# A two-layer graph and expert kernel: counting tables moved from setup into the first front stage, x loaded in pieces, aggregation in column halves, another finishing order

## The chip, the cores and the metric

One core of a Trainium2 chip runs the whole program. The metric is the device time in microseconds (us) of one execution; lower is better. The engines are named as the profile names them: PE is TensorE (PEld its weight loads), DVE is VectorE, ACT is ScalarE, POOL is GpSimd, SP is SyncE; a q behind a name (SPq, ACTq) is the engine's own sequencer, which also issues DMAs. L456 is line 456 of the kernel before.

## The reference

A graph of 3750 nodes and 60000 edges sorted by destination goes through two layers. x has 512 features for each node, 8 heads of 64.

```python
def gat_multihead(h, src, dst, Wfc, Wa):
    z = jnp.einsum('ni,hoi->nho', h, Wfc)
    e = leaky_relu(s_src[src] + s_dst[dst])          # s_*: z times a_src / a_dst, per head
    ex = jnp.exp(e - segment_max(e, dst)[dst])
    alpha = ex / segment_sum(ex, dst)[dst]
    return segment_sum(alpha[:, :, None] * z[src], dst).reshape(N, 512)
...
x = x + ffn(elu(gat(ln(x))) + ln(x))                 # layer 0: attention, FFN 512-256-512, layer norm
x = x + experts_choice(ln(x))                        # 16 experts, each takes its 468 best nodes
x = x + ln(gat1(ln(x), edge_type, edge_weight) + ln(x))
x = x + moe_top2(ln(x))                              # 8 experts, top 2 for each node
```

## The kernel before

The program is a row of stages, each with its own blocks and with a barrier at its end: setup, then for each layer front, aggregate and finish, and after them the expert stages. Nodes are held as 30 tiles of 128 rows; edges as 235 groups of 256 (J = 2 columns of 128), 15 groups for each of 16 chunks.

**setup** (L115 to L300). SP loads all of x (L168), then the edge lists, and writes -1e30 over the table first_scores in HBM (L174). POOL makes constants. DVE splits dst into a low and a high part, makes 30 pairs of one-hot matrices (L254, L255, each pair for 16 columns), and PE multiplies them (L295, 16 matmuls a pair) into a histogram of destinations. From this DVE works out first_edge (L259 to L269: the edge at which each node begins), then in 29 steps the group in which each tile ends (L272) and in 29 more the tables of the aggregation's steps (L278, L279): step_group, step_tile, group_freed, neg_base.

**front** (L335 on). SP loads the weights. DVE: stats of x in batches of 6 tiles (L474), normalise (L332), weights times attention vectors (L495, L496). PE turns the normalised tiles (L572) and scores them (L578), 16 columns a tile; DVE copies the scores out (L507, L508, the semaphore s_copied), makes a bf16 table of them (L513, L516) and, in layer 0, marks where a node's edges begin and end with six passes over the whole edge list (L524 to L529). Then PE does the big product z (L603, 4 matmuls of 512 columns a tile, each of which the trace shows as two instructions, as it does all f32 matmuls); ACT copies it out (L673) and SP stores it. Meanwhile POOL scatters 30 tiles of destination scores to first_scores (L456), one indirect DMA a tile, and then picks source scores for 5 groups of each chunk, 160 indirect DMAs (L464).

The remaining source scores are picked on PE, in a loop of m = 0 to 79: DVE makes one-hots (L553), PE selects from the table (L635, 6 matmuls), DVE masks (L562), PE spreads (L644, for m-1). Into this loop TURNS_AT puts 20 "turn blocks" (L625), transposes that bring scores to the form of the edges: ("g", i) for POOL's picks, ("d", n) for the scores read back from first_scores. ACT's order is: the z copies, wait for all of z, wait for all 30 scatters, 10 DMA issues that read first_scores back in 5 pairs (load_dst, L657), then one copy for each turn block (L685, and L690 at the end), with more load_dst pairs between. PE may not start turn block m (m > 0) before ACT has copied block m-1. After the loop: scans, exponentials and a turn back (alpha).

**aggregate** (L785 to L914), 264 steps. A step is one group of edges against one node tile. POOL gathers the z rows of a group with 2 indirect DMAs (L848), into 8 slots, SP passing on freed slots (L856). ACT prepares rel, alp and scale from alpha (L826, L828, L829) and evicts a bank of a finished tile (L814). DVE makes two one-hots (L879) and the messages (L882: gathered rows times alpha, which it reads from PSUM). PE opens a bank (L897), then for each of 2 columns multiplies one-hot by 512 message columns (L911) and, into a separate bank of denominators, by 8 alpha columns (L913). Four PSUM banks go round; LATE = 4 steps pass before a bank is evicted.

```python
for r in range(RING):
    t = pe.value_load(k.step_tile[0:1, bass.ds(i * RING + (r + LATE), 1)], ...)      # L906
    pe.wait_ge(evicted, i * RING + (r + LATE)); open_bank(...)
    pe.wait_ge(msg_ready, i * RING + (r + 3))
    # J times: matmul 512 columns (L911), matmul 8 columns (L913)
    mm.then_inc(summed, 1)
```

**finish_layer0**, 10 blocks of 3 tiles. DVE per block n: join (L1046, L1048), renew (L963), divide(n+2) (L1041), close(n) (L1053 to L1057, moments L936, then add_branch with the reciprocal L948 that needs ACT's root). ACT: renorm(n-1), norm(n+2) (L1087), expo(n+2) (L1092, L1093), hidden(n+1) (L1105), root(n) (L970, a square root), then the copies of x turns (L1098). PE: second(n) (L1179), y turn (L1155), hidden(n+1) (L1170), x turn (L1155), logits (L1187).

**experts0** ends with a block of its own that loads all of x again from x_rows (L1661).

Of the kernel before, what the change touches and what calls it, by code (L numbers as in the profile page):

```python
# [13 lines left out]
I32 = mybir.dt.int32  # L14
# [28 lines left out]
TURNS_AT = {**{4 + 4 * n: ("d", n) for n in range(GC - 1)}, 78: ("d", GC - 1), **{m: ("g", i) for i, m in enumerate((6, 13, 33, 53, 76))}}  # L43
# [6 lines left out]
NBK = 4  # L50
LATE = 4
# [63 lines left out]
def setup(k, I):  # L115

    nc = k.nc
    with ExitStack() as ctx:
        sem = lambda n: nc.alloc_semaphore(name="setup_" + n)
        sb = lambda n, s, d: ctx.enter_context(nc.sbuf_tensor("setup_" + n, s, d))  # L120
        loaded, x_padded, dve_done, pe_done, chain_sem, pool_chain = (
            sem("loaded"), sem("x_padded"), sem("dve_done"), sem("pe_done"), sem("chain"), sem("pool_chain"))
        d_filled, onehots_ready, onehots_used, table_read, table_stored = (
            sem("d_filled"), sem("onehots_ready"), sem("onehots_used"), sem("table_read"), sem("table_stored"))
        dst_i = sb("dst_i", [P, NG * J], I32)
        lo_i = sb("lo_i", [P, NG * J], I32)
        lo = sb("lo", [P, NG * J], BF16)
        hi = sb("hi", [P, NG * J], BF16)
        TO = 16
        oh_lo = sb("oh_lo", [P, 2, TO, P], BF16)  # L130
        oh_hi = sb("oh_hi", [P, 2, TO, NT], BF16)
        lowest = sb("lowest", [P, (EPAD + NPAD) * H // P], F32)
        hist = sb("hist", [P, NT], F32)
        incl = sb("incl", [P, NT], F32)
        first = sb("first", [P, NT], F32)
        dump = sb("dump", [P, NT], F32)
        empty = sb("empty", [P, NT], F32)
# [3 lines left out]
        kk = sb("kk", [P, STEPS], F32)  # L141
        g256 = sb("g256", [P, NGR - 1], F32)
        cmp = sb("cmp", [P, NGR - 1], F32)
        kt = sb("kt", [P, NT - 1], F32)
        ones_row = sb("ones_row", [P, NT], F32)
        steps_i = sb("steps_i", [P, 2, STEPS], I32)
        kg = sb("kg", [P, NT - 1], F32)
        group_at = sb("group_at", [P, NGR], F32)
        freed = sb("freed", [P, NGR], F32)
        ck = sb("ck", [P, STEPS], F32)  # L150
        q7 = sb("q7", [P, P], F32)
        spread_at = sb("spread_at", [P, HT * H + P], F32)
        src_i = sb("src_i", [P, NG * J], I32)
        part_i = sb("part_i", [P, 2, NG * J], I32)
        part = sb("part", [P, 2, NG * J], BF16)
        node_part = sb("node_part", [P, 2, NG * J], F32)
        upper = sb("upper", [P, NG * J], F32)
        parts_ready, parts_stored = sem("parts_ready"), sem("parts_stored")
        shifts = sb("shifts", [P, 30], I32)
        one_i = sb("one_i", [P, 30], I32)  # L160
        NOH = NG * J // TO

        with nc.Block() as block:
            @block.sync
            def _(sp):
                sp.wait_ge(x_padded, 1)
                sp.dma_start(k.x[:, 0:NT - 1, :], I["x"][0:(NT - 1) * P, :].rearrange("(t p) d -> p t d", p=P)).then_inc(loaded, 16)
                sp.dma_start(k.x[0:N - (NT - 1) * P, NT - 1, :], I["x"][(NT - 1) * P:N, :]).then_inc(loaded, 16)  # L168
                sp.dma_start(dst_i[:, :], I["dst_groups"]).then_inc(loaded, 16)
                sp.dma_start(k.src_groups[:, :], I["src_groups"]).then_inc(loaded, 16)  # L170
                sp.dma_start(k.src_chunks[:, :], I["src_chunks"]).then_inc(loaded, 16)

                sp.wait_ge(d_filled, 1)
                sp.dma_start(k.first_scores.rearrange("(p r) h -> p (r h)", p=P), lowest[:, :]).then_inc(table_stored, 16)  # L174
                sp.wait_ge(table_stored, 16)
                sp.dma_start(src_i[:, :], I["src_list"].rearrange("(p n) -> p n", p=P)).then_inc(loaded, 16)
                sp.wait_ge(loaded, 96)

            @block.gpsimd
            def _(pool):  # L180
                chain = Chain(pool, pool_chain)
                g = nc.gpsimd
                g.memset(k.x[:, NT - 1, :], 0.0).then_inc(x_padded, 1)
                g.memset(lowest[:, :], -BIG).then_inc(d_filled, 1)
                g.memset(k.ones[:, :], 1.0)
                g.memset(one_i[:, :], 1)
# [7 lines left out]
                g.iota(k.iota[:, :], pattern=[[1, P]], base=0, channel_multiplier=0, allow_small_or_imprecise_dtypes=True)  # L194
                g.iota(k.tile_iota[:, :], pattern=[[1, NT]], base=0, channel_multiplier=0, allow_small_or_imprecise_dtypes=True)
                g.iota(dump[:, :], pattern=[[P, NT]], base=EPAD, channel_multiplier=1, allow_small_or_imprecise_dtypes=True)
                g.iota(gate_i[:, :], pattern=[[0, 1]], base=0, channel_multiplier=1)
                g.iota(kk[:, :], pattern=[[1, STEPS]], base=0, channel_multiplier=0, allow_small_or_imprecise_dtypes=True)
                g.iota(g256[:, :], pattern=[[GE, NGR - 1]], base=GE, channel_multiplier=0, allow_small_or_imprecise_dtypes=True)
                g.iota(group_at[:, :], pattern=[[1, NGR]], base=0, channel_multiplier=0, allow_small_or_imprecise_dtypes=True)  # L200
                g.iota(spread_at[:, :], pattern=[[1, HT * H + P]], base=-HT * H, channel_multiplier=0, allow_small_or_imprecise_dtypes=True)
                g.iota(q7[:, :], pattern=[[0, CH], [1, H]], base=0, channel_multiplier=0, allow_small_or_imprecise_dtypes=True)
                g.iota(k.node[:, :], pattern=[[P, NT]], base=0, channel_multiplier=1, allow_small_or_imprecise_dtypes=True)
                chain(g.iota(shifts[:, :], pattern=[[-1, 30]], base=29, channel_multiplier=0))

        with nc.Block() as block:
            @block.sync
            def _(sp):

                sp.wait_ge(parts_ready, 1)  # L210
                sp.dma_start(k.src_key.rearrange("(p n) -> p n", p=P), part[:, 0, :]).then_inc(parts_stored, 16)
                sp.dma_start(k.src_tile.rearrange("(p n) -> p n", p=P), part[:, 1, :]).then_inc(parts_stored, 16)
                sp.wait_ge(parts_stored, 32)

            @block.vector
            def _(dve):
                v = nc.vector
                chain = Chain(dve, chain_sem)
                v.tensor_single_scalar(part_i[:, 0, :], src_i[:, :], P - 1, ALU.bitwise_and)
                chain(v.tensor_single_scalar(part_i[:, 1, :], src_i[:, :], 7, ALU.logical_shift_right))  # L220
                chain(v.tensor_copy(node_part[:, :, :], part_i[:, :, :]))
                chain(v.tensor_scalar(upper[:, :], node_part[:, 1, :], float(HT), None, ALU.is_ge))
                v.scalar_tensor_tensor(part[:, 0, :], upper[:, :], float(P), node_part[:, 0, :], ALU.mult, ALU.add)
                v.scalar_tensor_tensor(part[:, 1, :], upper[:, :], -float(HT), node_part[:, 1, :], ALU.mult, ALU.add).then_inc(parts_ready, 1)
# [110 lines left out]
def front(k, name, layer, I, w_dram, a_src_dram, a_dst_dram):  # L335
# [3 lines left out]
    with ExitStack() as ctx:  # L339
# [63 lines left out]
        with nc.Block() as block:  # L403
# [162 lines left out]
            def _(pe):  # L566
# [24 lines left out]
                for n in range(LEAD):  # L591
                    turn(n)
# [1510 lines left out]
```

## Time and profile before

| | |
|---|---|
| median of 3 runs | 4148.77 us (4142.35 to 4155.31) |
| profiled execution, own time | 4150.25 us |
| its span | 4148.7 us |
| mean granted PE clock | 0.868 |
| PE busy | 3108.9 us (75%) |
| DVE busy | 2261.3 us (55%) |
| POOL busy | 1616.9 us (39%) |
| ACT busy | 1099.6 us (27%) |

By the stretches of the timeline the stages lie so: setup 0 to 172 us, front of layer 0 to 636 (its second block from 571), aggregate 636 to 1290, finish_layer0 to 1583, choice of tokens and experts to 2309, front of layer 1 2311 to 2779, aggregate 2780 to 3430, the rest to 4149. A share of busy time is a mean over stages that have different limits, so it says little about any one edit: each stage is read by itself.

### The profile page before, as it was taken

The numbers are of one execution on the slowest core, as the hardware profiler recorded it, in microseconds if no ns is written. First come the engines' busy times: TensorE is split into PE (matmuls) and PEld (weight loads), VectorE is DVE, ScalarE is ACT, GpSimd is POOL, SyncE is SP. The second block draws the span as 40 slices with busy tenths as digits, with TensorE's granted clock in tenths as the row PEclk, the third lists the DMA queues.
The fourth block names the chain that finished last, engine by engine and source line by source line (L and its number), as shares of the span: only waits on it lengthen the run. The fifth ranks groups of instructions, "written<-read, shape, count | busy, mean of one in ns | idle before, by whom it ended". The sixth has DMA issues, their size and how long they took to land. (4 is left out here: it accounts for less than half of the span.)

```text
span 4148.7 us, 59841 instructions
## 1 busy us (share of the span) xinstructions
PE 3108.9 (75%) x12040; PEld 1861.1 (45%) x12041; DVE 2261.3 (55%) x4019; ACT 1099.6 (27%) x3080; POOL 1616.9 (39%) x1660
## 2 busy tenths in 40 slices
PE   1298958999997773389998599939999994308990
PEld 1174524555554552354444554515555553305660
DVE  6841577777776665731111413587777779712224
ACT  0021003444444440011111110014444444204440
POOL 0037706766761000013333067317776650140116
PEclk9999978999998785579999589969999995559995
DMA  2115616766662110035554426417666654053326
GB/s 106 35 43 130 172 39 178 203 192 195 192 192 71 53 56 29 0 106 154 144 156 101 130 72 152 121 37 210 199 196 193 193 163 183 23 214 133 121 106 226
DMA packets 334037, 541.05 MB, mean 130 GB/s; under 512 B 173220, under 2 KB 178596, under 8 KB 333168
## 3 DMA queue, kind: packets, MB, share of 16 engines
q0 software_dynamic: 118624, 327.53, 28.1%
q1 hardware_dynamic: 91472, 208.44, 14.5%
q10 hardware_dynamic: 123840, 3.94, 1.7%
q8 instruction: 40, 0.66, 0.1%
q14 instruction: 61, 0.50, 0.0%
HBM read 427.14 MB, written 112.61 MB: 130 GB/s over the span
## 5 line engine op out<-in xcount | busy, mean ns | idle before, releaser
L911 PE MATMUL bank<-aggregate_msg,aggregate_onehot 128*128 128x512 f32 x2112 | 1163.8, 639 | 20.4 <-issue 8.4
L848 POOL DMA_INDIRECT aggregate_zg<-z_rows,src_groups x940 | 890.4, 947 | 602.0 <-issue 267.9
L882 DVE TENSOR_TENSOR aggregate_msg<-aggregate_zg,bank 128x1024 f32<-128x1024 f32 x528 | 638.4, 1209 | 4.5 <-SPq L860 4.5
L913 PEld LDWEIGHTS bank<-aggregate_alp,aggregate_onehot 128*128 128x128 f32 x2112 | 402.4, 191 | 507.4 <-issue 507.4
L879 DVE TENSOR_SCALAR aggregate_onehot<-bank,aggregate_rel 128x128 f32<-128x128 f32 x1056 | 321.6, 346 | 362.2 <-PE bank L913 355.4
L814 ACT COPY acc<-bank x536 | 314.2, 586 | 358.0 <-issue 349.7
L464 POOL DMA_INDIRECT front_d<-src_scores,src_chunks x320 | 304.7, 952 | 97.6 <-issue 97.6
L1561 POOL DMA_INDIRECT exp_xg<-hn_rows,exp_gather_tok x64 | 67.0, 1048 | 705.1 <-DVE exp_gather_tok L1585 540.8
L911 PEld LDWEIGHTS bank<-aggregate_msg,aggregate_onehot 128*128 128x128 f32 x2112 | 318.8, 191 | 35.7 <-issue 28.7
L913 PE MATMUL bank<-aggregate_alp,aggregate_onehot 128*128 128x8 f32 x2112 | 300.8, 215 | 0.0
L826 ACT ACTIVATE aggregate_rel<-dst_groups,neg_base 128x2 f32 x528 | 156.0, 295 | 394.8 <-PE bank L913 288.2
L635 PE MATMUL bank<-front_w,front_table 128*120 128x512 bf16 x960 | 240.5, 388 | 9.0 <-DVE front_w L553 9.0
L456 POOL DMA_INDIRECT first_scores<-s_dst,first_edge x60 | 82.0, 1366 | 403.7 <-DVE s_dst L508 386.0
L1652 PE MATMUL bank<-exp_w,exp_h_t 128*117 128x512 f32 x512 | 222.5, 592 | 0.7 <-ACT exp_h_t L1619 0.7
L1644 PE MATMUL bank<-exp_xg_t,exp_w 128*128 128x468 f32 x512 | 206.0, 561 | 0.6 <-ACT exp_xg_t L1612 0.6
L635 PEld LDWEIGHTS bank<-front_w,front_table 128*120 128x120 bf16 x960 | 130.1, 136 | 153.3 <-issue 101.8
L603 PE MATMUL bank<-front_w,front_edge 128*128 128x512 f32 x360 | 169.4, 608 | 0.0
L644 PE MATMUL bank<-front_z,spread 120*128 120x512 f32 x320 | 166.3, 601 | 0.1
L572 PE MATMUL bank<-ident,front_early 128*128 128x128 f32 x240 | 64.7, 429 | 125.2 <-DVE front_early L332 105.6
L1572 POOL DMA_INDIRECT x_rows<-exp_y,exp_add_tok x64 | 101.2, 1581 | 141.9 <-DVE exp_y L1600 106.8
L1867 POOL DMA_DIRECT2D slot_out<-exp_y x66 | 35.8, 542 | 303.0 <-DVE exp_y L1884 303.0
L1644 PEld LDWEIGHTS bank<-exp_xg_t,exp_w 128*128 128x128 f32 x512 | 98.1, 192 | 106.8 <-issue 105.8
(365 smaller groups left out, 4356.1 us busy)
## 6 DMA issues: line engine op xcount, KB each, us to landing
exp_w<-in_L_ffn_w SPq DMA_DIRECT2D x32, 1024.0 KB, 8.2
slot_in<-alpha SPq DMA_DIRECT2D x1, 16896.0 KB, 43.5
exp_xin<-slot_in SPq DMA_DIRECT2D x66, 256.0 KB, 2.8
slot_out<-exp_y POOLq DMA_DIRECT2D x66, 256.0 KB, 2.3
z_rows<-front_z SPq DMA_DIRECT2D x60, 256.0 KB, 2.0
aggregate_zg<-z_rows,src_groups POOLq DMA_INDIRECT x940, 3.7
front_early<-src_key SPq DMA_DIRECT2D x16, 640.0 KB, 4.7
front_early<-src_tile SPq DMA_DIRECT2D x16, 640.0 KB, 4.5
```

The source lines that it names most:

```text
L464: pool.indirect_dma_start(picked[:, at:at + H], None, k.src_scores[:, :], bass.IndirectOffsetOnAxis(k.src_chunks[:, n:n + 1], 0)).then_inc ...
L603: mm = nc.tensor.matmul(k.ps[3 + n % 2][:, :], hn_t(c, slice(n * P, (n + 1) * P)), w[:, c, :], start=(c == 0), stop=(c == KC - 1))
L635: mm = nc.tensor.matmul(k.ps[5 + m % 2][0:HT * H, :], parts[:, part, half, :], onehot[:, m % OH, half, :], start=(part == 0 and half == 0) ...
L644: nc.tensor.matmul(sums[b], k.spread[0:HT * H, at:at + P], masked[0:HT * H, (m - 1) % 2, :], start=(c == 0), stop=(c == CH - 1)).then_inc( ...
L814: nc.scalar.copy(k.acc_all[:, bass.ds(t, 1), :].rearrange("p a d -> p (a d)"), flat[:, bass.ds(((t + (NBK - 1)) & (NBK - 1)) * 512, 512)]) ...
L848: pool.indirect_dma_start(zg[:, r, j, :], None, k.z_rows[:, :], bass.IndirectOffsetOnAxis(k.src_groups[:, n:n + 1], 0)).then_inc(gathered[ ...
L879: v.tensor_scalar(onehot[:, m, j, :], lanes, rel[:, r, j:j + 1], None, ALU.is_equal)
L882: v.tensor_tensor(msg[:, m, :, :].rearrange("p j (h d) -> p (j h) d", h=H), z, bcast_last(scale[r % 2], DH), ALU.mult).then_inc(msg_ready, 1)
L911: nc.tensor.matmul(flat[:, bass.ds((t & (NBK - 1)) * 512, 512)], onehot[:, m, j, :], msg[:, m, j, :], start=False, stop=True, skip_group_c ...
L913: mm = nc.tensor.matmul(flat[:, bass.ds(t * H + den, H)], onehot[:, m, j, :], alp[:, r, j * H:(j + 1) * H], start=False, stop=True, skip_g ...
L1644: mm = nc.tensor.matmul(k.ps[f][:, 0:CAP], w1[:, u, c, f * P:(f + 1) * P], xg_t[:, c, :], start=(c == 0), stop=(c == KC - 1))
L1652: mm = nc.tensor.matmul(k.ps[4 + q][0:PQ, :], h_t[:, f, q * PQ:(q + 1) * PQ], w2[:, u, f, :], start=(f == 0), stop=(f == F - 1))
```

## The change

Six edits, in one step:

- setup keeps only constants. In layer 0 the histogram, first_edge and the step tables are made inside front: one-hots and count matmuls lie among the z matmuls, count_ends and count_steps in the loop over m (at m = 4 to 32 and m = 35 to 63). The fill of first_scores is issued in front too, from z's buffer.
- front loads x itself, in 5 pieces of 6 tiles, and each batch of stats waits for its piece, in both layers. The block that loads x again after experts0 is gone.
- POOL makes 96 of its 160 picks first, then the 30 scatters, then the other 64 picks. TURNS_AT is another. ACT's order is the same.
- aggregate: the message row is 4 pieces of 260 columns (256 of message, 4 of alpha), so a step has 4 matmuls of 260 columns and none of 8; tiles alternate between two pairs of banks, and an eviction comes one step after (LATE = 1). ACT makes no rel and no alp; DVE's one-hot takes step_base and dst_groups at addresses from a register.
- the denominators are in acc_all, so their reciprocal waits for the last eviction.
- finish_layer0: ACT's order is root(n), hidden(n+1), expo(n+2), norm(n+2); DVE's close is split into receive (before divide) and close; PE does second(n+1) right after hidden(n+1).

```diff
-TURNS_AT = {**{4 + 4 * n: ("d", n) for n in range(GC - 1)}, 78: ("d", GC - 1), **{m: ("g", i) for i, m in enumerate((6, 13, 33, 53, 76))}}
+PICKS_BEFORE = 3
+TURNS_AT = {**{19 + 4 * n: ("d", n) for n in range(GC - 1)}, 76: ("d", GC - 1), **{m: ("g", i) for i, m in enumerate((4, 9, 14, 34, 50))}}
-LATE = 4
+LATE = 1
+HW = HD + H // 2
@@ front, SP
+                load_x(0)
                 sp.dma_start(w[:, :, :], ...)
...
+                for b in range(1, NT // SBT):
+                    load_x(b)
@@ front, POOL
+                if layer == 0:
+                    nc.gpsimd.memset(k.x[:, NT - 1, :], 0.0).then_inc(x_padded, 1)
+                    nc.gpsimd.memset(z[:, :, :], -BIG).then_inc(filled, 1)
+                    pool.wait_ge(lists_loaded, 32)
+                pool.wait_ge(s_stored, 16)
+                for i in range(PICKS_BEFORE):
+                    pick(i)
+                if layer == 0:
+                    pool.wait_ge(first_ready, 1)
+                    pool.wait_ge(table_filled, 16)
+                for n in range(NT):
+                    pool.indirect_dma_start(k.first_scores[:, :], ...)
+                for i in range(PICKS_BEFORE, GS):
+                    pick(i)
@@ front, DVE, layer 0
+                    for b in range(NOH):
+                        if b >= 2:
+                            dve.wait_ge(onehots_used, b - 1)
+                        v.tensor_tensor(oh_lo[:, b % 2], ..., ALU.is_equal)
+                        v.tensor_tensor(oh_hi[:, b % 2], ..., ALU.is_equal).then_inc(onehots_made, 1)
+                    dve.wait_ge(onehots_used, NOH)
...
+                    chain(v.tensor_copy(k.first_edge[:, :], first))
+                    dve.sem_inc(first_ready, 1)
                     (the six passes over the edge list follow)
                 for m in range(PICKS + 1):
+                    if layer == 0 and 4 <= m < 4 + NT - 1:
+                        count_ends(m - 4)
+                    if layer == 0 and 5 + NT <= m < 5 + NT + NT - 1:
+                        count_steps(m - 5 - NT)
@@ front, PE
+                    if layer == 0 and n >= 4:
+                        count(n - 4)
...
+                    for b in range(NT - 4, NOH):
+                        count(b)
+                    pe.wait_ge(first_ready, 1)
@@ aggregate, ACT
+                def evict(n): ... act.wait_ge(summed, n + (RING - 1)); copy(acc_all[t*2 : +2], banks[((t+1)&1)*2 : +2, 0:HW])
+                def prepare(n, r): ... act.wait_ge(summed, n + (RING - MS + 1)); copy(msg[.., HD:HW], coef); copy(scale[r % 2], coef)
                     for r in range(RING):
                         evict(i * RING + r)
+                        prepare(i * RING + (r + 1), r + 1)
@@ aggregate, PE
-                        pe.wait_ge(evicted, i * RING + (r + LATE))
-                        open_bank(bass.ds(((t + 1) & (NBK - 1)) * 512, 2))
                         pe.wait_ge(msg_ready, i * RING + (r + 3))
                         for j in range(J):
-                            nc.tensor.matmul(..512 columns..); nc.tensor.matmul(..8 columns..)
+                            for half in range(2):
+                                nc.tensor.matmul(k.banks[:, bank(t, half), 0:HW], onehot[:, m, j, :], msg[:, m, j * 2 + half, :], ...)
+                        pe.wait_ge(evicted, i * RING + (r + 3))
+                        open_tile(t + 1).then_inc(summed, 1)
@@ finish_layer0, ACT
-                    if n + 2 < NB:
-                        norm(n + 2)
-                        expo(n + 2)
+                    root(k, act, std[:, :], mv[:, :, 1], var_ready, std_ready, n)
                     if n + 1 < NB:
                         hidden(n + 1)
-                    root(k, act, std[:, :], mv[:, :, 1], var_ready, std_ready, n)
+                    if n + 2 < NB:
+                        expo(n + 2)
+                        norm(n + 2)
@@ finish_layer0, DVE
+                    receive(n)
                     if n + 2 < NB:
                         divide(n + 2)
                     close(n)
@@ experts0
-        with nc.Block() as block:
-            @block.sync
-            def _(sp):
-                sp.dma_start(k.x[:, :, :], k.x_rows.rearrange("(t p) d -> p t d", p=P)).then_inc(b_loaded, 16)
```

## Rows read from the trace of the kernel before

**Rows 1.** Busy time by stretch: us and instructions of each engine, PE clock, DMA share, GB/s.
```profile
0.00:33.00 33.00, 0.00 (x0) 0.01 (x1) 0.02 (x1) 0.02 (x1) 7.49 (x23) 1.00 0.86 318
...
266.00:372.00 106.00, 106.00 (x242) 46.71 (x241) 31.03 (x13) 16.99 (x29) 84.84 (x66) 1.00 0.29 88
372.00:571.00 199.00, 183.06 (x681) 99.25 (x680) 103.97 (x240) 10.32 (x26) 118.85 (x125) 0.96 0.60 153
...
2296.00:2308.00 12.00, 0.00 (x0) 0.00 (x0) 0.00 (x0) 0.00 (x0) 0.00 (x0) 0.50 1.05 387
```

**Rows 2.** Timeline of DVE in setup: start, us, operation.
```profile
122.29 2.28 DVE L254 TENSOR_TENSOR setup_oh_lo<-setup_lo,iota_bf 128x2048 bf16<-128x2048 bf16 x1
124.49 0.65 DVE L255 TENSOR_TENSOR setup_oh_hi<-setup_hi,iota_bf 128x480 bf16<-128x480 bf16 x1
```

**Rows 3.** One line's instructions in setup: duration ns min/median/max, first and last start.
```profile
L279 DVE SCALAR_TENSOR_TENSOR setup_ck<-setup_kk,setup_kt,setup_ck x29: 473/475/476, 144.4 to 169.3; 128x264 f32<-128x264 f32 x29
```

**Rows 4.** Timeline of DVE in the front of layer 0.
```profile
172.81 3.66 DVE L474 BATCH_NORM_STATS2 front_bn<-x 128x6 f32<-128x512 f32 x6 [1.04 <-PEq L2042]
...
266.33 0.41 DVE L507 COPY s_src<-bank 128x240 f32<-128x240 f32 x1 [12.70 <-PE bank L578]
...
268.81 4.20 DVE L524 TENSOR_TENSOR front_e<-front_wide 128x3840 bf16<-128x3840 int32 x1
...
295.44 2.16 DVE L529 TENSOR_SCALAR front_wide<-front_wide 128x7680 bf16<-128x7680 bf16 x1
```

**Rows 5.** Timeline of POOL over the same stretch, with the idle time before each.
```profile
274.15 3.77 POOL L456 DMA_INDIRECT first_scores<-s_dst,first_edge  x1 [0.30 <-issue]
...
298.72 0.96 POOL L456 DMA_INDIRECT first_scores<-s_dst,first_edge  x1 [0.30 <-issue]
```

**Rows 6.** Timeline of the loop over m, all engines.
```profile
396.93 0.69 PE L625 MATMUL bank<-ident,front_edge 128*128 128x128 f32 x2 [8.55 <-DMA front_edge<-first_scores]
...
404.69 2.87 ACTq L657 DMA_DIRECT2D front_edge<-first_scores  x2
...
449.73 0.75 DVE L562 SCALAR_TENSOR_TENSOR front_z<-front_edge,half_tile,bank 120x512 f32<-120x512 bf16 x1 [1.13 <-PE bank L635]
...
454.02 0.75 DVE L562 SCALAR_TENSOR_TENSOR front_z<-front_edge,half_tile,bank 120x512 f32<-120x512 bf16 x1 [0.84 <-PE bank L635]
```

**Rows 7.** Aggregate, 700 to 1200 us: waits (us in total, times, longest).
```profile
ACT acc L814 <- issue: 137.6, 207, 0.7
...
POOL aggregate_zg L848 <- SPq L856: 40.9, 25, 2.1
```

**Rows 8.** Timeline of aggregate around 1000 us.
```profile
1000.29 0.59 ACT L814 COPY acc<-bank  x1 [0.66 <-issue]
...
1001.47 1.12 PE L911 MATMUL bank<-aggregate_msg,aggregate_onehot 128*128 128x512 f32 x2
...
1002.57 0.68 PE L911 MATMUL bank<-aggregate_msg,aggregate_onehot 128*128 128x512 f32 x1
```

**Rows 9.** Costliest groups of the page: count, busy us, mean ns, idle before.
```profile
L848 POOL DMA_INDIRECT aggregate_zg<-z_rows,src_groups x940 | 890.4, 947 | 602.0 <-issue 267.9
L882 DVE TENSOR_TENSOR aggregate_msg<-aggregate_zg,bank 128x1024 f32<-128x1024 f32 x528 | 638.4, 1209 | 4.5 <-SPq L860 4.5
```

**Rows 10.** PE's sequencer at the step's register load, both layers.
```profile
L906 PEldq TENSOR_LOAD <-step_tile x528: 296/302/510, 639.1 to 3423.1; - x176
```

**Rows 11.** Timeline of PE in finish_layer0.
```profile
1512.71 5.43 PE L1170 MATMUL bank<-alpha,fin_w 128*128 128x384 f32 x16 [0.67 <-ACT alpha L1098]
```

**Rows 12.** What DVE's L948 waited for (us, times), whole trace.
```profile
  ACT fin_std L970: 62.6, 9
```

**Rows 13.** Busy time by stretch in finish_layer0, columns as in rows 1.
```profile
1473.30:1500.80 27.50, 20.79 (x77) 13.75 (x77) 19.29 (x31) 14.40 (x20) 0.00 (x0) 0.81 0.15 57
```

**Rows 14.** The timeline where the front of layer 1 begins.
```profile
2286.91 0.39 SPq L1661 DMA_DIRECT2D x<-x_rows  x1
...
2310.93 3.66 DVE L474 BATCH_NORM_STATS2 front_bn<-x 128x6 f32<-128x512 f32 x6 [40.72 <-PEq L2042]
```

More of the change, by code:

```diff
@@ L49 @@
 SLOTS = 8
-NBK = 4
-LATE = 4
+LATE = 1
+HD = D // 2
+HW = HD + H // 2
 AHEAD = 3
@@ L112, with setup @@
     pass
-def setup(k, I):
+def setup(k):
     nc = k.nc
@@ L405, in _, with load_x @@
             def _(sp):
+                def load_x(b):
+                    rows = I["x"] if layer == 0 else k.x_rows
+                    last = NT // SBT - 1
+                    full = SBT - 1 if layer == 0 and b == last else SBT
+                    sp.dma_start(k.x[:, b * SBT:b * SBT + full, :],
+                                 rows[b * SBT * P:(b * SBT + full) * P, :].rearrange("(t p) d -> p t d", p=P)).then_inc(x_loaded[b], 16)
+                    if layer == 0 and b == last:
+                        sp.wait_ge(x_padded, 1)
+                        sp.dma_start(k.x[0:N - (NT - 1) * P, NT - 1, :], rows[(NT - 1) * P:N, :]).then_inc(x_loaded[b], 16)
+                load_x(0)
                 sp.dma_start(w[:, :, :], w_dram.rearrange("(c p) n -> p c n", p=P)).then_inc(loaded, 16)
@@ L453, in _, with pick @@
             def _(pool):
-                pool.wait_ge(s_copied, 2)
-                for n in range(NT):
-                    pool.indirect_dma_start(k.first_scores[:, :], bass.IndirectOffsetOnAxis(k.first_edge[:, n:n + 1], 0),
-                                            k.s_dst[:, n, :], None).then_inc(scattered, 16)
-                pool.wait_ge(s_stored, 16)
-                for i in range(GS):
+                def pick(i):
                     for j in range(J):
@@ L472, in stats @@
                 def stats(b):
+                    dve.wait_ge(x_loaded[b], 32 if layer == 0 and b == NT // SBT - 1 else 16)
                     for j in range(SBT):
@@ L589, in spread_kinds, with count @@
                                      start=True, stop=True).then_inc(kinds_spread, 1)
+                def count(b):
+                    pe.wait_ge(onehots_made, b + 1)
+                    for t in range(TO):
+                        mm = nc.tensor.matmul(k.ps[5][:, 0:NT], oh_lo[:, b % 2, t, :], oh_hi[:, b % 2, t, :],
+                                              start=(b == 0 and t == 0), stop=(b == NOH - 1 and t == TO - 1))
+                    mm.then_inc(onehots_used, 1)
                 for n in range(LEAD):
@@ L801, in aggregate @@
         ROUNDS = STEPS // RING
[L802 to L805 removed]
+        lanes = k.ps[4][:, 0:P]
+        scale = [k.ps[5 + u][:, 0:J * H] for u in range(2)]
         zslots = zg[:, :, :, :].rearrange("p r j d -> p r (j d)")
@@ L2043, in stage @@
                 run(k, *args)
-        stage(setup, I)
+        stage(setup)
         for layer in range(2):
```

369 lines of the change are left out of this document (159 added, 210 removed).

## The prediction

> **What bounds the kernel now.** I read the busy shares first and then by stretch, since no engine is full over the whole span. Setup is DVE's: 30 pairs of one-hots, 2.28 + 0.65 us each [rows 2], after an x load that fills the DMA engines [rows 1]. The z stretch of front is PE's: 106 us busy of 106 [rows 1]. The loop over m is PE's too, 183 of 199 us; DVE has 104 us of work for 80 turns there, 1.3 us each, while the loop's period is (454.02 - 449.73)/2 = 2.15 us [rows 1, 6]. In aggregate no engine is full: 207 evictions in 500 us are 2.418 us a step [rows 7]. PE alone would need about 2.23: 1.10 us from column to column, twice, and the small opening [rows 8]. POOL needs 2 x (0.947 + 0.30) = 2.51 us a group, which over 235 groups and 264 steps is 2.23 a step [rows 5, 9], and was held by SPq for only 41 us in 500 [rows 7]. So the step is a ring: PE's step, DVE's message, ACT's 0.66 us of issue before 0.59 us of eviction [rows 8], PE again. In finish_layer0 a block lasts 27.5 us with DVE busy for 19.3 and PE for 20.8 [rows 13]; DVE waited for ACT's root 62.6 us in 9 blocks [rows 12].
>
> **Setup and the first front stage.** What stays of setup is constants, 7.5 us of POOL [rows 1]. Front's DVE began at 172.8 [rows 4] and would begin at 7.5: -165.3. x must now be loaded inside: before stats(1) can run, two pieces of 1.57 MB, 1.05 MB of weights and 0.52 MB of vectors land; at 387 GB/s [rows 1] that is 12.2 us and 2 for issue and latency, where stats(1) ran 4.1 after the start. That is +10; I take 10.3. Bounds: 4 (the first piece alone) and 20 (the whole of x). Scores were copied 93.5 us after the start [rows 4]: now at 111.3.
>
> Then the counting. PE does 16 small matmuls per z tile, an estimated 0.45 us with both kinds full, on top of 3.5 us a tile [rows 1]: 30 tiles end at about 229. DVE needs 2.28 + 0.65 = 2.93 less overlap, 2.77 a pair, so it keeps up. The last four counts and the 12 small operations to first_edge cost 12: 241.7. The six passes over the edges ran from 268.81 to 297.60, 28.8 us [rows 4], beside the z matmuls, which hid them. Now they come after the one-hots and stand open: 270.5. PE's first selection follows at 272.2, where before it was at 376.9. So on this path the gain is 105 us.
>
> **POOL's order gives part of it back.** POOL picks from about 114. The rows show what DVE does to it: a scatter took 3.77 us beside L524, which reads two inputs from SBUF and took 4.20, against 0.96 once the passes had ended [rows 4, 5]. The one-hots have that form too, so I take it that one pick can pass during a pair and one in the gap: 2 per 3.9 us. By 270.5 some 74 of 96 picks are out, the rest end at 298, 30 scatters of 1.26 us [rows 5] at 336, their last lands at 338.5. ACT stands at its wait for all scatters. Behind it are ten load_dst issues and then every turn copy. An issue took 1.44 us late in the loop [rows 6]: 14.4, so the first turn copy is at 353. PE may pass turn block 0 (m = 4) but not block 1 at m = 9, due 295.6: it waits 58 us. After it 71.5 turns of 2.157 us and 7 of tail (count_steps makes DVE's part 1.3 + 24.9/28 = 2.19 [rows 3], level with PE's, up to 3 us in 29 turns): 516, against 571.4. Front of layer 0: **-55**. Lower bound -90: POOL is not held, and the copy is at 317. Upper bound -30: the ten issues take 32 us, as in the first loop before, and DVE's count_steps shows in full.
>
> The Trainium skill bears on this in "SBUF — State Buffer", section "Who interferes with whom": it says that tensor_tensor has no 2-port mode and was not seen to stall a DMA's descriptors, since these need the write interface. By that POOL would run at 1.25 us a pick and the stage would gain 90. The 3.77 us rows speak against it, and the same section's sentence that two SBUF inputs contend with GpSimd reads agrees with them.
>
> **Layer 1's front.** The removed reload was issued 24.0 us before front began [rows 14]; 2 us of barrier stay: -21.8. The pieces cost +10.3 as above. There are no counts, but the order is the same: s is the time of the score copy. 96 picks, 30 scatters, landing and issues are 1.5 + 120.3 + 37.9 + 2.5 + 18 = s + 180. PE reaches m = 9 at s + 139.6, since the z stretch takes 116 us: 40 us of wait, and the loop ends near s + 343, where it ended at s + 304.6. In all -21.8 + 10.3 + 38.7 = **+27** (10 to 45, by how long the issues take: 14 to 32).
>
> **Aggregate, twice.** The columns per step are nearly the same: 8 instructions of 260 instead of 4 of 512 and 4 of 8. No row has 260; 384 columns took 5.43/16 = 0.339 us with the start [rows 11], 512 about 0.43, so cost goes with columns, an estimated 0.22: 8 x 0.22 + 2 small openings = 1.95 to 2.15 a step, against 2.23. DVE loses nothing, 0.69 + 1.21 [rows 9]. POOL is unchanged. The new ring has two tiles' banks, so it closes after two steps: step done, eviction 1.0 (0.59 of copy for 520 columns [rows 8], semaphore and addresses), PE's opening 0.35, its register load 0.30 + 0.15 and addresses 0.5 [rows 10], matmuls 2.15: 4.5 for two, 2.26 each. With the end of a round of six I take 2.31. That is (2.418 - 2.31) x 264 = 28.5 saved, less 1 because the reciprocal waits for the last copy: -27.5 a layer, **-55**. Bounds: POOL's 2.23 gives -50 a layer; from above, ACT's eviction and preparation stand in one line now (1.25 + 1.2 us), and if the opening waits for both the step is 2.45: +10 a layer.
>
> **finish_layer0.** ACT's root comes right after the turn copies, and DVE has divide and the next moments to do while it runs, so the 62.6 us can go. What is late next is PE: 20.8 us of work in 27.5 at a clock of 0.81 [rows 13]. DVE alone would give 20.3 with its small gaps. I take 22 to 25 a block, 45 of the 62.6 us: **-45** (-20 to -63). norm and expo, now last on ACT, are needed one block later.
>
> **Sum.** 4150.25 - 55 + 27 - 55 - 45 = 4022. The profiled execution is 1.5 us above the median, so 4021.
>
> **The rivals.**
> 1. *The forecast*: 3985 to 4060, 0.42.
> 2. *Aggregate runs at POOL's rate*, 235 x 2.51 + 8 = 597 us a stage. For it: the ring estimate is only 0.03 above. Against: the ring has two banks instead of four, and any jitter adds. It would give 50 more: 3972; 0.15.
> 3. *POOL is not held back by the one-hots*: front of layer 0 gains 35 more, 3986. Against: the 3.77 us rows; the gaps may let more picks through. 0.12.
> 4. *The ring is no shorter and PE in finish sits at the half clock*: aggregate 0, finish -20: 4101; 0.16.
> 5. *load_dst issues are slow in both fronts*, 32 us as before: 18 more twice: 4057; 0.09.
> 6. *Slower: the two-bank ring*. PE opens the next tile only after the eviction of the tile before, and the next step's matmuls stand behind that opening. If eviction, opening and register load do not overlap the matmuls at all the step is 2.15 + 0.5 to 2.15 + 2.3. All else gains 73 us, 0.138 for each of 528 steps: from 2.56 us a step the kernel is slower. At 2.70 it is 4150 - 73 + 149 = 4226. Against: PE's matmuls ran gapless through 1.10 us steps with register loads beside them [rows 8]. 0.06.
>
> The time is the first case's, 4021. The range 3950 to 4092 holds cases 1, 2, 3 and 5 and a third of case 4. A measurement of this kernel tells 0.3%, 12 us, from no change; only case 6, and a sliver of case 4 with a bad front, reach that: faster 0.92, same 0.02, slower 0.06.
>
> **What would show each step.** Front of layer 0: s_copied near 111, first_edge near 241, the first selection near 272; picks of 2 to 3 us beside the one-hots (right) or 0.95 (rival 3); one PE idle of some 58 us before a turn block, released by ACT's copy, and one of some 40 in layer 1. If ACT's wait is short, POOL's order costs nothing and the front gains up to 100. Aggregate: message starts 2.31 us apart; the wait POOL L848 on SPq grows if the ring binds and stays small if POOL does. Finish: blocks of 22 to 25 us, and no wait of DVE for the root. What would make the whole wrong is the ring's step: 0.1 us there is 53 us of time.

## The result and the profile after

The changed kernel takes 4043.4 us (median of 4 runs, 4041.56 to 4045.25) beside 4146.11 us of the kernel before: 0.9749 of its time, 95% interval 0.9731 to 0.9767. It is faster by 103 us; the forecast was 4021 us, in a range of 3950 to 4092. The profiled execution has a span of 4041.3 us at a mean clock of 0.844. On the chip of the first four experiments (e1 to e4) the kernel before took 5096.65 us, 23% longer, and every kernel's front and aggregate were longer there (aggregate of layer 0: 916 us in e4, which leaves that stage as it is, and not 635), so of these four only stages are read that kept their length. From here on a line number is that of the kernel whose trace is shown, and s is the time of the score copy in layer 1, as in the prediction.

By the first and last instruction of each stage (us; the idle time at a stage's ends goes with the stage that follows):

| stage | before | after | difference | forecast |
|---|---|---|---|---|
| setup and front of layer 0, to the start of aggregate | 636.2 | 582.1 | -54.1 | -55 |
| aggregate, layer 0 | 653.0 | 634.7 | -18.4 | -27.5 |
| finish_layer0 | 292.2 | 247.2 | -45.0 | -45 |
| end of experts0 to the start of the second aggregate | 502.0 | 522.7 | +20.7 | +27 |
| aggregate, layer 1 | 649.9 | 634.6 | -15.3 | -27.5 |
| the rest (the stages not edited) | | | +5 | 0 |

The page's costliest groups, as in [rows 9] (count, busy us, mean ns, idle before and what ended it):

```profile
L905 PE MATMUL bank<-aggregate_msg,aggregate_onehot 128*128 128x260 f32 x4224 | 1038.6, 396 | 213.4 <-issue 130.9
L837 POOL DMA_INDIRECT aggregate_zg<-z_rows,src_groups x940 | 888.6, 945 | 654.9 <-POOLq L2034 323.7
L871 DVE TENSOR_TENSOR aggregate_msg<-aggregate_zg,bank 128x1024 f32<-128x1024 f32 x528 | 644.0, 1220 | 221.3 <-ACT bank L814 198.2
```

The gathers cost what they did; the message now waits 198 us in all for ACT's preparation, where it hardly waited.

DVE in the front of layer 0, as [rows 4]:

```profile
111.03 0.41 DVE L419 COPY s_src<-bank 128x240 f32<-128x240 f32 x1 [12.71 <-PE bank L554]
...
241.18 0.18 DVE L473 CAST first_edge<-front_d 128x30 int32<-128x30 f32 x1
241.51 4.16 DVE L479 TENSOR_TENSOR front_e<-front_wide 128x3840 bf16<-128x3840 int32 x1 [0.15 <-DVE first_edge L473]
...
268.09 2.16 DVE L484 TENSOR_SCALAR front_wide<-front_wide 128x7680 bf16<-128x7680 bf16 x1
```

Scores copied at 111.0 (forecast 111.3), first_edge at 241.4 (241.7), the passes done at 270.3 (270.5).

POOL beside the one-hots, and beside the passes, as [rows 5], with DVE's pair of one-hots above it:

```profile
150.83 2.29 DVE L456 TENSOR_TENSOR front_e<-front_d,iota_bf 128x2048 bf16<-128x2048 bf16 x1 [1.06 <-PE bank L570]
153.04 0.65 DVE L457 TENSOR_TENSOR front_e<-front_d,iota_bf 128x480 bf16<-128x480 bf16 x1
...
151.57 2.37 POOL L359 DMA_INDIRECT front_d<-src_scores,src_chunks  x1 [0.30 <-issue]
154.24 0.94 POOL L359 DMA_INDIRECT front_d<-src_scores,src_chunks  x1 [0.30 <-issue]
155.49 2.37 POOL L359 DMA_INDIRECT front_d<-src_scores,src_chunks  x1 [0.30 <-issue]
...
258.98 9.31 POOL L359 DMA_INDIRECT front_d<-src_scores,src_chunks  x1 [0.30 <-issue]
```

Two picks in 3.92 us. One of them ends at 153.94, when both one-hots of the pair are done (153.69).

PE in the loop over m of layer 0, then the same place in layer 1:

```profile
293.05 1.46 PE L627 MATMUL bank<-front_w,front_table 128*120 128x512 bf16 x6
356.07 0.66 PE L617 MATMUL bank<-ident,front_d 128*128 128x128 f32 x2 [61.56 <-ACT front_e L679]
...
2454.49 0.66 PE L617 MATMUL bank<-ident,front_d 128*128 128x128 f32 x2 [40.46 <-ACT front_e L679]
```

And what ACT did ahead of that copy:

```profile
343.10 12.36 ACTq L649 DMA_DIRECT2D front_edge<-first_scores  x10
355.56 0.37 ACT L679 COPY front_e<-bank 128x256 f32<-128x256 f32 x1 [126.12 <-issue]
```

The releaser of PE's 61.56 us is named as ACT's copy. But ACT had run nothing for 126 us before that copy: in its order the ten issues come first, and before them its wait for POOL's 30 scatters. The tenth issue, and not the copy, is what m = 9 waits for.

Aggregate, 700 to 1200 us, as [rows 7], and the sequencer's load, as [rows 10]:

```profile
ACT acc L805 <- PE bank L891: 276.7, 211, 2.0
...
DVE aggregate_msg L871 <- ACT bank L814: 84.8, 106, 0.8
PE bank L905 <- issue: 55.7, 80, 1.0
POOL aggregate_zg L837 <- SPq L845: 32.8, 33, 2.0
```

```profile
L901 PEldq TENSOR_LOAD <-step_tile x528: 296/302/489, 584.4 to 3314.6; - x176
```

211 evictions in 500 us are 2.37 us a step (2.418 before, 2.31 forecast). Most of PE's wait is put down to "issue": nothing that the profile shows holds it, and that is where its own sequencer is to be looked at.

Around 1000 us, as [rows 8]:

```profile
1001.26 0.19 PE L891 MATMUL bank<-zero_bf 128*128 128x2 bf16 x2
...
1001.80 0.59 ACT L805 COPY acc<-bank  x1 [0.83 <-PE bank L891]
...
1002.48 2.02 PE L905 MATMUL bank<-aggregate_msg,aggregate_onehot 128*128 128x260 f32 x8 [1.03 <-issue]
...
1004.33 0.19 PE L891 MATMUL bank<-zero_bf 128*128 128x2 bf16 x2
```

The opening at 1001.26 lets ACT copy at 1001.80; PE's next step starts 1.03 us idle after its last work, and ends with an opening at 1004.33.

finish_layer0 as one stretch, columns as in [rows 13]:

```profile
1218.00:1465.00 247.00, 202.25 (x760) 129.31 (x760) 194.27 (x291) 142.77 (x197) 0.00 (x0) 0.81 0.20 72
```

DVE's L941, the reciprocal that had waited 62.6 us for the root [rows 12], now waits for nothing. The length of this stage depends on the granted clock. The same stage of the same code in e4 and in e9:

```profile
1576.70:1829.10 252.40, 207.26 (x760) 132.44 (x760) 194.69 (x292) 142.91 (x197) 0.00 (x0) 0.78 0.19 70
1197.40:1438.80 241.40, 196.37 (x760) 126.50 (x760) 194.05 (x292) 142.78 (x197) 0.00 (x0) 0.83 0.20 73
```

Between the two the mean clock is 0.78 and 0.83, PE's busy time differs by 10.9 us and the stage by 11.0; DVE's differs by 0.6.

### The profile page after: what moved, and what is told of

Its sections match the earlier page's. It is cut to its first block and busy times, and to the rows that moved or that the text cites. A ratio compares the mean times of both kernels' runs of the same rounds, so it can differ in the third digit from the quotient of the medians.

```text
span 4041.3 us, 61866 instructions
## 1 busy us (share of the span) xinstructions
PE 2913.9 (72%) x12568; PEld 2012.7 (50%) x12569; DVE 2339.0 (58%) x4017; ACT 1007.9 (25%) x2552; POOL 1651.9 (41%) x1655
## 5 line engine op out<-in xcount | busy, mean ns | idle before, releaser
L905 PE MATMUL bank<-aggregate_msg,aggregate_onehot 128*128 128x260 f32 x4224 | 1038.6, 396 | 213.4 <-issue 130.9
L905 PEld LDWEIGHTS bank<-aggregate_msg,aggregate_onehot 128*128 128x128 f32 x4224 | 761.9, 190 | 329.7 <-issue 236.0
L359 POOL DMA_INDIRECT front_d<-src_scores,src_chunks x320 | 370.8, 1159 | 327.1 <-DMA src_scores<-s_src 230.2
L866 DVE TENSOR_SCALAR aggregate_onehot<-bank,step_base,dst_groups 128x128 f32<-128x128 f32 x1056 | 383.4, 405 | 38.9 <-PE bank L891 24.4
L627 PE MATMUL bank<-front_w,front_table 128*120 128x512 bf16 x960 | 238.6, 385 | 36.2 <-DVE front_w L519 36.2
L528 DVE SCALAR_TENSOR_TENSOR front_z<-front_early,half_tile,bank 120x512 f32<-120x512 bf16 x80 | 59.8, 747 | 163.3 <-PE bank L627 163.3
L1649 PEld LDWEIGHTS bank<-exp_w,exp_h_t 128*117 128x117 f32 x512 | 91.4, 181 | 120.7 <-issue 119.2
L891 PEld LDWEIGHTS bank<-zero_bf 128*128 128x128 bf16 x1060 | 103.8, 98 | 88.9 <-issue 9.6
L813 ACT COPY aggregate_msg<-alpha 128x16 f32 x530 | 108.0, 204 | 119.2 <-issue 40.8
```

Source lines behind the costliest of these rows:

```text
L359: pool.indirect_dma_start(picked[:, at:at + H], None, k.src_scores[:, :], bass.IndirectOffsetOnAxis(k.src_chunks[:, n:n + 1], 0)).then_inc ...
L627: mm = nc.tensor.matmul(k.ps[5 + m % 2][0:HT * H, :], parts[:, part, half, :], onehot[:, m % OH, half, :], start=(part == 0 and half == 0) ...
L813: nc.scalar.copy(msg[:, r % MS, :, HD:HW], coef.rearrange("p (u h) -> p u h", u=J * 2))
L866: v.tensor_scalar(onehot[:, m, j, :], lanes, k.step_base[:, bass.ds(i * RING + r, 1)], k.dst_groups[:, bass.ds(g * J + j, 1)], ALU.add, AL ...
L905: nc.tensor.matmul(k.banks[:, bank(t, half), 0:HW].rearrange("p a n -> p (a n)"), onehot[:, m, j, :], msg[:, m, j * 2 + half, :], start=Fa ...
L1649: mm = nc.tensor.matmul(k.ps[4 + q][0:PQ, :], h_t[:, f, q * PQ:(q + 1) * PQ], w2[:, u, f, :], start=(f == 0), stop=(f == F - 1))
```

## The experiments

**e3 and e4: one edit undone each.** e3 has finish_layer0 as before. e4 loads x again after experts0, whole, in the block that was there before, and the pieces stay in layer 0 alone:

```diff
-                load_x(0)
+                if layer == 0:
+                    load_x(0)
...
                 def stats(b):
-                    dve.wait_ge(x_loaded[b], 32 if layer == 0 and b == NT // SBT - 1 else 16)
+                    if layer == 0:
+                        dve.wait_ge(x_loaded[b], 32 if b == NT // SBT - 1 else 16)
...
+                sp.dma_start(k.x[:, :, :], k.x_rows.rearrange("(t p) d -> p t d", p=P)).then_inc(b_loaded, 16)
```

> Changed kernel with finish_layer0 as it was before. Theory (the new order is worth 45 us, by itself): 45 us slower than the changed kernel, about 4088 us, and VectorE waits for the root again some 60 us. Rival (part of the shorter stage came from the layout of the sums that aggregate leaves, or from TensorE's clock): under 35 us.

> Changed kernel with the old load of all of x between the experts of layer 0 and the front of layer 1; the pieces stay in layer 0. Theory (the reload block costs 21.8 us, the pieces inside front give back 10.3): 11 us slower than the changed kernel, about 4054 us. Rival (the time of the pieces is lost wherever x is loaded): no difference within 4 us.

Their whole times are 4887.05 and 4855.4 us, on the first chip, where the changed kernel was not run: the forecasts of 4088 and 4054 us can't be tested as they stand. In e3 the stage took 291.1 us, against 247.2, 251.9 and 252.4 in e1, e2 and e4, which have the new order and ran on that same chip: 39 to 44 us come from the order. At the nearest clocks, 0.77 in e3 and 0.78 in e2 and e4, it is 39. The wait is back to the digit (us, times):

```profile
  ACT fin_std L963: 62.6, 9
```

In e4 the time from the last instruction of experts0 to the score copy of layer 1 was 2652.7 - 2526.6 = 126.1 us. In e1, e2 and e3 on the same chip it was 115.3, 115.4 and 115.2, and in the changed kernel 2277.5 - 2162.9 = 114.6. So to load x in pieces there is worth 11 us, for a forecast of 21.8 less 10.3. e4's front begins 24 us behind the load:

```profile
2535.22 0.39 SPq L1661 DMA_DIRECT2D x<-x_rows  x1
2559.09 0.38 SPq L287 DMA_DIRECT2D front_w<-in_L_gnn_WT  x1
```

**e1 and e1b: ScalarE's order in front.**

```diff
-TURNS_AT = {**{19 + 4 * n: ("d", n) for n in range(GC - 1)}, 76: ("d", GC - 1), **{m: ("g", i) for i, m in enumerate((4, 9, 14, 34, 50))}}
+TURNS_AT = {**{36 + 3 * n: ("d", n) for n in range(GC)}, **{m: ("g", i) for i, m in enumerate((4, 9, 14, 58, 74))}}
...
-                act.wait_ge(scattered, 16 * NT)
-                for m in range(DR):
-                    load_dst(m)
...
                 for m, (kind, n) in enumerate(turn_order):
+                    if (kind, n) == ("d", 0):
+                        act.wait_ge(scattered, 16 * NT)
+                        for first_n in range(DR):
+                            load_dst(first_n)
```

> Changed kernel, with ScalarE's order in front altered in both layers: the copies of POOL's first three turn blocks come before the wait for all scatters and the ten issues that read the scores back, and the blocks of read-back scores stand at m = 36, 39, ... 78, POOL's at 4, 9, 14, 58, 74. Theory (TensorE's 61.6 us stall at m = 9 in layer 0 is ScalarE's queue behind the scatters, and layer 1 has some 40 us of the same): both stalls go, the time falls by 85 to 105 us to about 3945 us. Rival (the stall only moves, to the read-back transfers or to POOL's late picks): a wait of 20 us or more stands at m = 36 or m = 74 in layer 0 and the gain is under 60 us. Second rival (front is set by POOL's 190 indirect DMAs and not by the order): no more than 10 us of gain in layer 1.

> The kernel of e1_turns again, on another chip. ScalarE copies POOL's first three turn blocks before it waits for the scatters, and the read-back blocks stand at m = 36 to 78. Theory: the 61.6 us stall of layer 0 and some 40 us of layer 1 go, the loop over m runs at 2.16 us a turn: about 3945 us, 85 to 105 us less than the changed kernel. Rival (the stall moves): gain under 60 us, with a wait of 20 us or more at m = 36 or m = 74.

e1 took 4846.74 us on the first chip, 0.9517 of the kernel before there, and its front says nothing by itself. e1b took 3948.29 us beside 4147.81 of the kernel before: 0.9521, interval 0.9505 to 0.9537, 95 us under the changed kernel. Front of layer 0 ends at 519.7 and not 580.4, front of layer 1 lasts 469.7 and not 512.2: 60.7 and 42.5 us, the two stalls. No wait of 20 us stands at m = 36 or m = 74. What PE still waits in the loop of layer 0 is the start, for DVE's passes over the edges, and 3.6 us at the turn blocks:

```profile
PE bank L627 <- DVE front_w L519: 32.5, 1, 32.5
...
PE bank L617 <- issue: 3.6, 1, 3.6
```

**e9: that order without the new places.** TURNS_AT as in the changed kernel.

> Changed kernel with ScalarE's order of e1b alone: POOL's first turn copies before the wait for the scatters, TURNS_AT as in the changed kernel, where the first read-back block stands at m = 19. Theory (both the order and the places count): in layer 0 TensorE passes m = 9 and 14 and then waits at m = 19, from about 314 to about 350 instead of from 294 to 356, some 36 us; in layer 1 the read-back lands near s + 172 and m = 19 comes at s + 158, a wait of some 15 instead of 40 us. So about 50 of the 95 us, near 3993 us. Rival (the order does it all, the places in the loop are of no account): within 10 us of 3948. Rival (the places do it all): within 10 us of 4043.

4002.53 us (0.9658, 0.9642 to 0.9675): 41 us gained, not 95, and not none. PE's wait has moved to m = 19 and has another releaser, the read-back:

```profile
347.14 0.69 PE L617 MATMUL bank<-ident,front_edge 128*128 128x128 f32 x2 [26.95 <-DMA front_edge<-first_scores]
```

Front of layer 0 ends 20.6 us earlier than in the changed kernel (at 559.8), front of layer 1 is 20.7 us shorter. Layer 0 still loses 40 us against e1b. 27 of them are the wait at m = 19, where I expected 36. PE waits 10.6 us more in three places (2.5, 1.7 and 6.4 us), each at a block of POOL's picks: the rows at 309.0, 385.1 and 427.2 us read front_d. e1b has 3.6 us of that kind, and some 6 us stay unassigned.

**e7: POOL's old order in layer 1 alone.**

```diff
+                pool.wait_ge(s_stored, 16) if layer == 0 else pool.wait_ge(s_copied, 2)
+                before = PICKS_BEFORE if layer == 0 else 0
-                for i in range(PICKS_BEFORE):
+                for i in range(before):
                     pick(i)
...
+                if layer == 1:
+                    pool.wait_ge(s_stored, 16)
-                for i in range(PICKS_BEFORE, GS):
+                for i in range(before, GS):
                     pick(i)
```

> Changed kernel with POOL's old order in layer 1 alone: 30 scatters as soon as the scores are copied, then all 160 picks; TURNS_AT and ScalarE's order as in the changed kernel. Theory (in layer 1 TensorE waits at m = 9 because 96 picks stand ahead of the scatters): the wait of some 40 us at m = 9 goes; picks of group 2 then end near s + 162 us where m = 14 comes at s + 147, so some 15 us of wait stand there instead: about 25 us faster than the changed kernel, near 4018 us. Rival (the order of POOL doesn't matter, the ten issues of ScalarE do): within 5 us of the changed kernel.

4019.69 us (0.9697, 0.9681 to 0.9713), 24 us under the changed kernel as forecast. The 40.46 us stall is gone, and another of 12.7 us, for POOL's third group, stands in the stage:

```profile
PE bank L620 <- issue: 12.7, 1, 12.7
```

Front of layer 1 lasts 488.4 us and not 512.2. So 24 of the 32 us that layer 1 lost behind its score copy came from the 96 picks ahead of the scatters.

**e8: the compared numbers in PSUM.** This is the disputed hold on POOL, by itself.

```diff
+                    v.tensor_copy(k.ps[7][:, 0:P], k.iota)
...
-  v.tensor_tensor(oh_lo[:, b % 2], bcast_last(lo_hi[:, 0, at], P), k.iota_bf[:, :].unsqueeze(1).to_broadcast([P, TO, P]), ALU.is_equal)
+  v.tensor_tensor(oh_lo[:, b % 2], bcast_last(lo_hi[:, 0, at], P), k.ps[7][:, 0:P].unsqueeze(1).to_broadcast([P, TO, P]), ALU.is_equal)
```

> Changed kernel with one edit in the front of layer 0: the row of numbers that the one-hots are compared with lies in PSUM (f32), not in SBUF, so these VectorE operations read one input from SBUF and not two. Theory (an operation with two inputs from SBUF holds POOL's indirect DMA until it ends): the picks beside the one-hots take 0.95 us each and not 2.37, all 96 are out by 238, the scatters then wait for first_edge at 241, five of them are held by the passes over the edges, the rest end near 302: the first turn copy comes at 317 and not 354, the stall of TensorE at m = 9 is 25 and not 61.6 us, the time 4007 us (35 less than the changed kernel). Rival (the page's rule: the write interface is what is held, or the load on the DMA queues makes the picks slow): picks stay at 2.37 us every second time, no gain; if VectorE reads PSUM more slowly, up to 10 us are lost.

A one-hot and the picks beside it, and then the scatters beside the passes over the edges, which are as they were:

```profile
197.97 2.29 DVE L457 TENSOR_TENSOR front_e<-front_d,bank 128x2048 bf16<-128x2048 bf16 x1 [1.07 <-PE bank L571]
...
199.52 0.94 POOL L359 DMA_INDIRECT front_d<-src_scores,src_chunks  x1 [0.30 <-issue]
200.77 0.94 POOL L359 DMA_INDIRECT front_d<-src_scores,src_chunks  x1 [0.30 <-issue]
202.02 0.94 POOL L359 DMA_INDIRECT front_d<-src_scores,src_chunks  x1 [0.30 <-issue]
...
241.71 4.86 POOL L373 DMA_INDIRECT first_scores<-s_dst,first_edge  x1 [5.04 <-DVEq L475]
...
250.90 7.82 POOL L373 DMA_INDIRECT first_scores<-s_dst,first_edge  x1 [0.30 <-issue]
...
268.60 2.49 POOL L373 DMA_INDIRECT first_scores<-s_dst,first_edge  x1 [0.30 <-issue]
```

Every pick beside the one-hots takes 0.94 or 0.95 us, the one-hots take 2.29 us as before, and the stall at m = 9 is 26.6 us (forecast 25). Front of layer 0 is 36.2 us shorter (forecast 35), which puts aggregate's start 90.3 us before that of the kernel before, the -90 of the prediction's lower bound. The whole, 4014.54 us (0.9685, 0.9669 to 0.9701), is 29 us shorter. In the Trainium skill, "SBUF — State Buffer", section "Who interferes with whom", two sentences differ: that two inputs from SBUF contend with GpSimd's reads, and that tensor_tensor was not seen to stall a DMA's descriptors. On this kernel the first holds for indirect DMAs: 2.37 us with two inputs from SBUF, 0.94 with one. The edit changes the place of that input and its type too (bf16 to f32), and no run parts the two. Two inputs are also not the only form that goes with a held DMA: the last two passes are TENSOR_SCALAR with one input, and the scatter beside the second of them took 2.49 us (the pick there 2.46 in the changed kernel), where a free one takes 0.97.

**e2 and e2b: the register load out of the ring.**

```diff
-                        t = pe.value_load(k.step_tile[0:1, bass.ds(i * RING + (r + LATE), 1)], ...)
+                        t = pe.value_load(k.step_tile[0:1, bass.ds(i * RING + (r + LATE), 1)], ...) if r == 0 else t_next
...
+                        if r + 1 < RING:
+                            t_next = pe.value_load(k.step_tile[0:1, bass.ds(i * RING + (r + 1 + LATE), 1)], ...)
                         pe.wait_ge(evicted, i * RING + (r + 3))
```

> Changed kernel, with one edit in aggregate: for five steps of each round of six, TensorE's sequencer loads the next step's tile number before it waits for the eviction, not after. Theory (the step is a ring over two steps: eviction end, 0.63 us to the register load, 0.31 us of load, 0.69 us to the first matmul, 2.04 us of matmuls and opening, 0.35 us to the copy, 0.59 us of copy; 4.61 us for two): the load leaves the ring, two steps take 4.3 us, the step falls from 2.37 to 2.25 us, where POOL's 2.23 us begin to bind; about 25 to 30 us less in each of two stages, 50 to 60 in all. Rival (the message chain ScalarE preparation, VectorE message, TensorE is the ring): no change, under 10 us. Rival (POOL already sets it): no change.

> The kernel of e2_load_first again, on another chip. TensorE loads the next step's tile number before it waits for the eviction. Theory (a ring over two steps, 4.61 us, of which 0.31 us of load and some of its 0.35 us of address work leave): the step falls from 2.37 to about 2.25 us, 25 to 30 us a stage, about 3985 us in all. Rivals (the message chain, or POOL, sets the step): under 10 us in all.

e2 took 4863.77 us on the first chip (0.9523) and its aggregate, some 905 us, says nothing. e2b took 3974.44 us (0.958, 0.9564 to 0.9596), 69 us under the changed kernel, and each aggregate 598.3 us and not 634.6. Its waits between 700 and 1200 us:

```profile
ACT acc L805 <- PE bank L891: 251.7, 215, 2.1
...
DVE aggregate_msg L871 <- SPq L849: 72.0, 125, 0.9
```

The message waits for gathers now (L849 is where SP passes a gathered group on), hardly for ACT any more (5.7 us), and POOL has no wait for a free slot in that window: the stage has come to POOL's 235 x 2.51 + 8 = 597 us. It ends at 1179, so 215 evictions in 479 us are 2.23 us a step, not 2.25, and the gain is 36 us a stage where I had expected 25 to 30. The edit leaves the message chain as it is, so neither that chain nor POOL set the step before.

**e6: both.**

> Both edits together. Theory: they lie in different stages, so their gains add: about 145 to 155 us under the changed kernel, near 3895 us. Rival: one stage hands its gain back at its barrier or by TensorE's clock: the sum is short by 15 us or more.

3868.74 us (0.9327, 0.9311 to 0.9343): 175 us under the changed kernel, where 145 to 155 were forecast and the two edits alone gave 95 + 69 = 164. By stages they add up: 103 us in the two fronts (e1b) and 73 in the two aggregates (e2b) alone, 174 in these four stages together. No stage gives back what another gained. It beats both kernels, by 4.3% and 6.7%.

## Why the prediction was right, point by point

**The front of layer 0** came out as it was summed: -54.1 for -55. Scores, first_edge and passes lie within 0.3 us of their places, POOL's rate beside the one-hots is the two picks in 3.9 us, and the loop over m ends at 516.2 (516 forecast). Small errors cancel on the way. Front begins at 5.4 us and not 7.5, and the pieces cost 12.1 us and not 10.3. The picks are out at 303.6 and not 298, since the passes held single picks for up to 9.31 us and let only five through; the scatters follow, and ACT may issue at 343.1 (338.5 forecast). Its ten issues then took 12.4 us and not 14.4, so the wait is 61.6 for 58. e8 shows the hold on POOL by taking it away, e1b the queue of ACT behind the scatters. The third rival (POOL not held) is refuted. The fifth (slow issues of 32 us) too: they took 12.4 us, and 11.7 in layer 1. That the counting itself, moved into front, is worth the 105 us of its path is read from these places in time; no run moves it back alone.

**The front of layer 1**: +20.7 for +27. The wait is 40.5 for 40, the pieces 11.5 for 11.5 (11 in e4). The 6 us between lie in the term "the loop ends at s + 343": it ended at 2613.4, which is s + 335.9. PE reached m = 9 at s + 136.5 and not s + 139.6, and was released at s + 177.0 and not s + 180, so both ends of the wait came 3 us early and its length was right. From there to the loop's end it took 158.9 us, where 163 were forecast.

**finish_layer0**: -45.0 for -45, and e3 shows that it is the order. The forecast of 22 to 25 us a block holds too. The joins (L1046 before, L1039 after) of blocks 0 and 1 stand together, 10.2 us apart in both kernels. From the second join to the tenth, eight blocks, it is 1308.8 to 1530.0 before and 1236.3 to 1413.5 after: 27.65 and 22.15 us a block, single blocks after from 19.7 to 24.3. DVE is busy for 19.3 of them and is held directly by PE for 4.8 us in the eight blocks, and by ACT's exponentials, second root and normalised rows for 15.1; ACT's own waits there are for PE (65 us at L1166 and L1151). That PE is late next is what the traces at different clocks show: in the ten traces with this order the stage is 241.4 to 252.4 us long, and PE's busy time goes with it from 196.4 to 207.3, while DVE's stays at 194.1 to 194.7. The hit to the digit is luck: at the clock of 0.78 of other traces the same code gives -40, at 0.83 it gives -51. Whether the order itself raises the clock (0.76 before) is not shown.

**Aggregate**: -33.7 for -55, the one term that was mis-sized by much, and it makes nearly all of the 22 us by which the forecast was low. The mechanism was right, a ring over two steps with the register load in it. In the 220 steps between the 30th and the 250th the load began 0.63 us after an eviction's end, PE's first matmul 0.69 us after the load's end (medians; never sooner than 0.65), and the eviction 0.35 us after the opening. The ring is 0.63 + 0.31 + 0.69 + 2.04 + 0.35 + 0.59 = 4.61 us for two steps, where I had 4.5. The size that was wrong is the way from the eviction's end to the first matmul: 1.63 us, where I had 0.35 + 0.30 + 0.15 + 0.5 = 1.30; matmuls and eviction were a little shorter than forecast. With the longer step at the end of each round of six it is 2.37 a step, where I had 2.31: 0.06 us, 528 times, or 32 us. Against that the stage's ends gave back 7.7 us in both layers together where I had them cost 2: behind the loop there were four evictions with LATE = 4 and there is one now, and from the last eviction inside the loop to the end of the stage it is 6.9 us and not 10.0. The fourth rival (no gain from the ring) and the sixth (over 2.56 us a step) did not come; the second, POOL's rate, came only with e2b's edit, at the 597 us that it was priced at. No run undoes the parts of this edit one by one (columns in halves, ACT's shorter preparation, LATE), so which of them made the step 0.05 us shorter than before is open.

**The clock** in the two profiled executions fell from 0.868 to 0.844 on average; PE stands 102 us in the two stalls, and no stage that was not edited moved by more than 2.5 us. Together they cost some 5 us, which the forecast had at 0.

## What to carry to other kernels

In a queue that is written by hand, ask of each wait what stands behind it that has no need of it: here ACT waited for scatters before it copied blocks that had nothing to do with them. The order alone gave 41 us (e9), and with the places in the loop moved along 95 (e1b). In a ring of few stages every sequencer instruction between a wait and the next release counts: a load of 0.3 us placed after the wait, with the address work behind it, cost 36 us in a stage of 264 steps. And a move of work off the critical path must be followed on the engines beside it: the counting took 0.49 us of PE for each z tile (3.92 us from one to the next, where it was 3.43) and cost POOL 1.4 us for each pair of one-hots.

## What was not expected of the hardware

- Beside a one-hot comparison on DVE, 128 x 2048 bf16 with both inputs in SBUF, an indirect DMA of POOL took 2.37 us; with one input in PSUM the comparison took the same 2.29 us and the DMA 0.94.
- On the chip of e1 to e4 the kernel before took 5096.65 us and not 4147.81, e1 4846.74 and not 3948.29 (e1b), e2 4863.77 and not 3974.44 (e2b): 22 to 23% longer. In the traces of e1 to e4 the extra time lies in front and aggregate alone; the other stages kept their times within some 5 us. The cause is open: many of the waits there are put down to "remote" (144 us of ACT's evictions between 900 and 1400 us in e4), and nothing in these traces shows what lies behind it.
- The profile puts PE's wait for its own sequencer down as "issue", and it had to be worked out from the sequencer's rows (0.30 us of load, then 0.69 to the first matmul).
